# Macaron block with a Mamba2 scan on one core: gate tanh ahead of norms in the opening, the maxima's bank free with their copy, gate weights counted apart, conv copies ahead of the second norm

## The reference

```python
x = x + 0.5 * ffn(layernorm(x))          # first FFN
x = x + block(layernorm(x))              # h = y + mamba2(rmsnorm(y)), then h + mlp(rmsnorm(h))
x = x + 0.5 * ffn(layernorm(x))          # closing FFN, same weights

def ffn(x):    # W = (q - zeros) * scales in groups of 64, 512 x 512
    return x @ W.T + (x @ lora_A.T) @ lora_B.T / 16 + bias
def mamba2(h):
    z, xBC, dt = split(h @ w_in.T)       # 512 | 128 + 128 + 512 | 4 columns
    xBC = silu(causal_conv_4_taps(xBC) + conv_b); dt = softplus(dt + dt_bias)
    Y = scan over chunks of 128 tokens, 4 heads, state 128 x 128 per head
    return ((Y + D * x) * silu(z)) @ w_out.T
def mlp(h):
    return (silu(h @ gate_w.T) * (h @ up_w.T)) @ down_w.T      # 1792 wide
```

## Time and profile before

| | before |
|---|---|
| median of 3 runs | 795.04 us (794.87 to 795.27) |
| profiled execution | 794.72 us |
| span in its trace | 793.0 us |
| mean granted clock of TensorE | 0.987 |
| PE busy | 762.4 us, 96% |
| DVE, ACT, POOL busy | 628.0, 448.0, 335.8 us |

### The profile page before, as it was taken

The page is one execution under the profiler, slowest core; times in us unless marked ns, Lnnn a source line. Parts: engine busy times, 40 slices in busy tenths (PEclk is TensorE's granted clock), DMA queues, the critical chain, the costliest instruction groups (busy, mean ns, idle before and its releaser), DMA issues.

```text
span 793.0 us, 10650 instructions
## 1 busy us (share of the span) xinstructions
PE 762.4 (96%) x3470; PEld 355.1 (45%) x3470; DVE 628.0 (79%) x1235; ACT 448.0 (57%) x881; POOL 335.8 (42%) x392
## 2 busy tenths in 40 slices
PE   8899799999999889989997999999999999999998
PEld 3444354454455445434443444444444444444443
DVE  7798568978867877787799787887878878767994
ACT  4876656776775756544436455545645555534441
POOL 5631334563543268764614125125224224223674
PEclk9999899999999989999999899999999999999999
DMA  8832653542331111620151354644544643443655
GB/s 303 182 67 53 136 91 79 94 107 54 80 68 27 41 27 27 126 41 20 31 129 28 80 119 72 129 100 82 139 81 80 146 80 68 79 81 67 120 159 133
DMA packets 95415, 71.86 MB, mean 91 GB/s; under 512 B 65233, under 2 KB 72401, under 8 KB 95361
## 3 DMA queue, kind: packets, MB, share of 16 engines
q0 software_dynamic: 17280, 31.46, 22.2%
q1 hardware_dynamic: 77600, 39.66, 20.0%
q10 hardware_dynamic: 480, 0.07, 0.1%
HBM read 20.32 MB, written 4.19 MB: 31 GB/s over the span
## 4 chain that ended last, share of the span: by engine, by line
PE 70%; DVE 15%; ACT 6%; issue 3%; POOL 3%; DMA 2%; ACTq 0%; DVEq 0%; POOLq 0%
PE PS L1936 61%; PE PS L2059 3%; DVE raw L1447 2%; DVE st L1278 1%; PE PS L2067 1%; DVE state L1429 1%; PE PS L2158 1%; DMA x_t<-hb 1%; PE PS L2032 1%; PE PS L2041 1%; DVE w_in L1545 1%; ACT xds L833 1%; DVE stage L1447 1%; POOL r L520 1%; DVE xs L1379 1%
## 5 line engine op out<-in xcount | busy, mean ns | idle before, releaser
L1936 PE MATMUL PS<-h,w_in 128*128 128x512 f16 x480 | 111.5, 385 | 7.2 <-DVEq L1503 4.4
L711 POOL DMA_DIRECT2D xs<-x x59 | 50.9, 863 | 153.1 <-ACT x L1151 139.4
L1936 PE MATMUL PS<-h,x_t 128*128 128x512 f16 x408 | 94.0, 379 | 0.2 <-DVE pre L1780 0.2
L1936 PEld LDWEIGHTS PS<-h,w_in 128*128 128x128 f16 x480 | 47.3, 99 | 74.7 <-issue 18.3
L1936 PE MATMUL PS<-n_T,stage 128*128 128x512 f16 x288 | 71.5, 379 | 0.0
L1151 ACT ACTIVATE x<-PS,d_d 128x512 f32<-128x512 f32 x59 | 40.2, 681 | 38.6 <-PE PS L1936 38.6
L1936 PEld LDWEIGHTS PS<-h,x_t 128*128 128x128 f16 x408 | 39.5, 98 | 48.9 <-issue 2.7
L520 POOL TENSOR_TENSOR r<-mv,mhalf 128x1 f32<-128x1 f32 (+1 forms) x32 | 28.5, 891 | 70.6 <-DVE mv L1282 54.1
L711 POOL DMA_DIRECT2D xs<-n x29 | 25.2, 869 | 74.7 <-ACT n L1151 65.2
L1121 ACT ACTIVATE xds<-tm,dgh 128x512 f32<-128x512 f32 x24 | 17.3, 722 | 56.7 <-DVE tm L1867 56.7
L1936 PE MATMUL PS<-pre,stage 128*128 128x512 f16 x192 | 49.3, 379 | 0.0
(11 more groups left out here) (314 smaller groups left out, 1812.4 us busy)
## 6 DMA issues: line engine op xcount, KB each, us to landing
xs<-x POOLq DMA_DIRECT2D x75, 256.0 KB, 3.3
xs<-n POOLq DMA_DIRECT2D x29, 256.0 KB, 3.3
x_t<-x_in SPq DMA_DIRECT2D x16, 256.0 KB, 3.0
x_t<-hb POOLq DMA_DIRECT2D x16, 256.0 KB, 3.8
out<-x_t SPq DMA_DIRECT2D x16, 256.0 KB, 2.3
raw_gu<-gate_t SPq DMA_DIRECT2D x7, 512.0 KB, 4.4
raw_gu<-up_t SPq DMA_DIRECT2D x7, 512.0 KB, 6.5
raw_d<-down_t SPq DMA_DIRECT2D x7, 512.0 KB, 7.7
```

Source lines behind the costliest of these rows:

```text
L711: po.dma_start(chunk_of(xs, c), d_tmps[d % 3], accum_op=ALU.add).then_inc(s_acc[d % 3], 16)
L1936: ins = pe.matmul(out_, lhs(a, b, k), rhs(a, b, k), start=first and n == 0, stop=last and n == len(todo) - 1)
```

## The change

Five edits of order and counting; no operation on data is added or removed.

1. In the opening, ACT takes `hi0(8)` and the tanh of the gate blocks earlier, ahead of the norm `hi1(7)`; DVE takes `lo0(8)` and `silu_z` earlier, ahead of `lo1(6)` and `lo1(7)`.
2. Also in the opening, DVE's `max_row(1)` stands ahead of `x1_stats(3)`.
3. The bank of the first pair's maxima is freed by the copy out of it (`scale_read`, first count of e_scx) and no longer by the end of `scales` (e_wscale). The copy stands in step 10 ahead of `lo2` and `advance` on DVE, and `bound_spread(0)` ahead of `w(10)` and `csm(3)` on PE.
4. In steps 2, 6 and 10 ACT's conv copies (`slot_a` of the slot's first block) stand ahead of `hi1`, `scan2` and `renorm`.
5. For pairs 1 to 6 the gate weights are counted apart: ACT counts the high half of the gate by itself, DVE makes its low half in `st_g` and the other low halves in `st_a`, which in the last unit of a pair stands after the unit's u4 and c22 sums; PE waits for the gate at IP1 and for the rest at IP6.

```diff
@@ -285,6 +285,7 @@
+        W_HI_G = [4 * p - 1 for p in range(NP)]
@@ -307,7 +308,7 @@
             if c == 2 * CH + 2:
-                put(("mx", 0), (e_wscale, 1))
+                put(("mx", 0), (e_scx, 1))
@@ -945,6 +946,8 @@ ACT, step(c)
                     scan_decay(c + 1, (c + 1) % CH)
+                if j == 2 and i + 1 < NS:
+                    slot_a(i + 1, SLOTS[j][0])
                 if a < NCH:
                     hi1(a, a % CH)
@@ -955,7 +958,8 @@ ACT, step(c)
                 if i + 1 < NS:
-                    slot_a(i + 1, SLOTS[j][0])
+                    if j != 2:
+                        slot_a(i + 1, SLOTS[j][0])
                     slot_b(i + 1, SLOTS[j][0])
@@ -994,15 +998,15 @@ ACT, prologue
                 tanh(0, 4)
+                hi0(8, 0)
                 tanh_z(0, 0)
                 tanh(0, 5)
+                tanh_z(0, 1)
                 scan_ecs(0, 0)
                 scan1(0, 0)
                 scan_decay(0, 0)
-                hi0(8, 0)
+                tanh_z(0, 2)
                 hi1(7, 3)
-                tanh_z(0, 1)
-                tanh_z(0, 2)
                 scan2(0, 0)
                 tanh_z(0, 3)
@@ -1067,7 +1071,9 @@ ACT, hi_st
                     ac.wait_ge(e_norm, p)
-                    ac.activation(g[:, 0, :, :], raw_gu[:, 0, :, cols], ACT.Copy)
+                    first = ac.activation(g[:, 0, :, :], raw_gu[:, 0, :, cols], ACT.Copy)
+                    if x == 0:
+                        first.then_inc(e_w_hi, 1)
@@ -1486,17 +1492,15 @@ DVE, the scales of a pair
...
+            def scale_read(p):
+                ve.wait_ge(e_all, 2 + p + 1)
+                scale_link(p, itertools.count(1))(ve.tensor_copy(mxa3[:, :], PS[:, mx_bank(p), P:P + 3]))
@@ -1523,22 +1527,31 @@ DVE, the low halves
...
+            def st_g(p):
+                ve.wait_ge(e_w_hi, W_HI_G[p])
+                lo_g(0).then_inc(e_w_gu0, 1)
             def st_a(p):
-                ve.wait_ge(e_w_hi, p * 3)
-                lo_st(0).then_inc(e_w_gu0, 1)
+                ve.wait_ge(e_w_hi, W_HI_G[p] + 1)
+                lo_sums(0).then_inc(e_w_gu0, 1)
@@ -1634,16 +1647,16 @@ DVE, prologue
                 silu(0, 4)
+                lo0(8, 0)
                 silu_z(0, 0)
                 silu(0, 5)
+                silu_z(0, 1)
+                prep0(9, 1)
                 lo1(6, 2)
-                lo0(8, 0)
                 weights(0, 0)
-                silu_z(0, 1)
+                silu_z(0, 2)
+                scan1(0, 0)
                 lo1(7, 3)
-                silu_z(0, 2)
-                prep0(9, 1)
-                scan1(0, 0)
                 silu_z(0, 3)
@@ -1677,6 +1690,8 @@ DVE, step(c)
+                if c == 2 * CH + 2:
+                    scale_read(0)
                 if c > 0:
                     lo2(c - 1)
@@ -1751,8 +1766,8 @@ DVE, opening
+            max_row(1)
             x1_stats(3, 3, B_P[1])
-            max_row(1)
@@ -1847,16 +1863,19 @@ DVE, unit(m)
                     if n == 3:
-                        st_a(p + 1)
+                        st_g(p + 1)
...
                 ve.tensor_tensor(c22[k], u3[k], p_bank(m, IP5), ALU.add).then_inc(e_add, 1)
+                if p + 1 < NP and n == 3:
+                    st_a(p + 1)
@@ -2126,10 +2147,11 @@ PE, step(c)
+                if c == 2 * CH + 2:
+                    bound_spread(0)
                 w(c)
                 if c == 2 * CH + 2:
                     csm(i + 1)
-                    bound_spread(0)
@@ -2280,7 +2302,7 @@ PE, unit(m)
                 if x == 0:
-                    pe.wait_ge(e_w_gu0, p + 1)
+                    pe.wait_ge(e_w_gu0, 2 * p)
@@ -2291,6 +2313,8 @@ PE, unit(m)
+                if x == 0:
+                    pe.wait_ge(e_w_gu0, 2 * p + 1)
                 seventh(m, IP6)
```

More of the change, by code:

```diff
@@ L1487, in bound_row, with scale_link @@
                 ve.tensor_scalar(mdg[:, :], ident[0:3, 0:3], mr[:, :], None, ALU.mult).then_inc(e_max1, 1)
-            def scales(p):
[L1490 to L1499, removed]
+            def scale_link(p, n):
+                return lambda ins: link(ins, e_scx, p * 5 + next(n))
+            def scale_read(p):
+                ve.wait_ge(e_all, 2 + p + 1)
+                scale_link(p, itertools.count(1))(ve.tensor_copy(mxa3[:, :], PS[:, mx_bank(p), P:P + 3]))
+            def scales(p):
+                power_of_two(pw3[:, :], sw3[:, :], mxa3[:, :], scale_link(p, itertools.count(2)))
                 if p > 0:
@@ L1516, in dn_lo @@
             def dn_lo(p):
-                ve.wait_ge(e_w_hi, p * 3 + 2)
+                ve.wait_ge(e_w_hi, W_HI_G[p] + 3)
                 hi, lo_ = (w_dn[p % 2][:, a, :, :] for a in range(2))
@@ L1524, in cut_b, with lo_g, lo_sums @@
                 dn_lo(0)
-            def lo_st(x):
+            def lo_g(x):
+                cols = slice(x * P, (x + 1) * P)
+                g = w_st[x][0]
+                return ve.tensor_tensor(g[:, 1, :, :], raw_gu[:, 0, :, cols], g[:, 0, :, :], ALU.subtract)
+            def lo_sums(x):
                 cols = slice(x * P, (x + 1) * P)
                 g, u, s_ = w_st[x]
-                ve.tensor_tensor(g[:, 1, :, :], raw_gu[:, 0, :, cols], g[:, 0, :, :], ALU.subtract)
-                ve.tensor_tensor(u[:, 1, :, :], raw_gu[:, 1, 2:4, cols], u[:, 0, :, :], ALU.subtract)
                 for n in range(2):
                     ve.tensor_tensor(s_[:, 1, n, :, :], s_tmp[n][:, :, cols], s_[:, 0, n, :, :], ALU.subtract)
-                return ve.tensor_tensor(s_[:, 1, 2:4, :, :], s34[:, :, :, cols], s_[:, 0, 2:4, :, :], ALU.subtract)
+                ve.tensor_tensor(s_[:, 1, 2:4, :, :], s34[:, :, :, cols], s_[:, 0, 2:4, :, :], ALU.subtract)
+                return ve.tensor_tensor(u[:, 1, :, :], raw_gu[:, 1, 2:4, cols], u[:, 0, :, :], ALU.subtract)
+            def st_g(p):
+                ve.wait_ge(e_w_hi, W_HI_G[p])
+                lo_g(0).then_inc(e_w_gu0, 1)
             def st_a(p):
-                ve.wait_ge(e_w_hi, p * 3)
-                lo_st(0).then_inc(e_w_gu0, 1)
+                ve.wait_ge(e_w_hi, W_HI_G[p] + 1)
+                lo_sums(0).then_inc(e_w_gu0, 1)
             def st_b(p):
-                ve.wait_ge(e_w_hi, p * 3 + 1)
-                lo_st(1).then_inc(e_w_gu1d, 1)
+                ve.wait_ge(e_w_hi, W_HI_G[p] + 2)
+                lo_g(1)
+                lo_sums(1).then_inc(e_w_gu1d, 1)
             def t_lo(q, r_):
@@ L1831, in unit @@
                 if p + 1 < NP and n == 2 and m > 2:
+                    scale_read(p + 1)
                     scales(p + 1)
@@ L1859, in unit @@
                     t_los(3, 0, 1, 2, 3)
+                    scale_read(2)
                     scales(2)
@@ L1897, in _ @@
             gate_up(0, EARLY_GU)
+            scale_read(1)
             scales(1)
@@ L1903, in _ @@
             down(0)
+            st_g(1)
             st_a(1)
```

## The result

| | before | changed |
|---|---|---|
| median | 795.12 us (794.87 to 795.27, 4 runs) | 782.76 us (782.02 to 784.74, 4 runs) |
| ratio | | 0.9849, 95% interval 0.9829 to 0.9868 |
| profiled execution, its span | 794.72, 793.0 us | 782.24, 780.5 us |
| mean granted clock | 0.987 | 0.998 |

The account below looks back on a forecast made before the run. PE, busy 96% of the span, was taken as the bound, with gains only in its pauses and clock. 4.6 + 0 + 0.1 + 3.3 + 5.0 = 13.0 off 794.72 gives 781.7, plus 0.3 for the median 782.0; range 777.5 to 787.0.

Parts of the forecast that it names:

- Which pauses cost clock: PE's pauses: four, of 2.20 to 4.43 us, cost about twice their waits; behind shorter ones no half clock.
- Opening: Opening up to the next stage's product: f(8) starts at 89.7, scores' pause gone, one clock fall charged; gain 4.6 us.
- one fall of the clock: Opening, behind the remaining 2.0 us pause before f(8): a 3.4 us stretch at half clock, costing 1.7 us.
- The rival without a fall: Opening: the 2.0 us pause before f(8) costs no clock; 14.7 us gained in all, 780.3 us; chance 25%.
- The early maximum: Opening, row maximum ahead of x1_stats(3): the pause only moves to ACT's norm of chunk 5; gain 0.
- half clock through close pauses: Early maximum: pauses before 36.92 and before the next product come close enough for a clock fall; 1.7 us to lose.
- Conv copies: Steps 2, 6 and 10: earlier ACT copies hardly help, as full DVE frees the next bank; 0.1 us, between 0 and 2.7.
- The maxima's bank: Step 10: the 4.43 us wait and half clock vanish, partly given back with DVE then the limit; gain 3.3 us.
- The heirs that were named: Behind step 10: PE then waits about 0.9 us on cs_b, and later on POOL's scores.
- The gate: Before pair 2: pause down 2.1 us to 1.5, and 2.9 us of half clock back; gain 5.0 us.
- Sum: Whole kernel: the five terms add to a gain of 13.0 us, giving a median of 782.0 us.

Follow-up runs that it names:

- the pause filled: Changed kernel with ten matmuls computing nothing needed in the pause before f(8), into the bank f(8) then overwrites: 781.42 us, ratio 0.9833.
- the scales later: Changed kernel with scales and descale of the first pair behind the copies of the decays on DVE in step 10: 783.90 us, ratio 0.9860.
- the opening alone: Kernel before with only the new order of the opening (part 1), plus a piece of part 5: 789.91 us, ratio 0.9931.

## Why the prediction was right, point by point

- **Which pauses cost clock.** The argument that the long pauses are worth about twice what their waits say held: of the 12.5 us of span 6.2 are busy time of PE. But "four pauses cost, the shorter ones don't" is a reading of one execution. Other executions show 2.65 without half clock, and 1.72, and even 1.20 followed by 0.69, with it, while the 1.5 before pair 2 and the 1.7 and 1.5 on residual2 have none in any profile. Where a page of the Trainium skill (TensorE: Matmul & The Clock Gate, section Why this matters for your kernels) speaks of gaps over about 3 us, the runs have half clock behind pauses of 1.2 to 2.7 in some executions.
- **Opening, 4.6 forecast, 4.1 measured.** The steps came as written: the bank free early, then the transpose last; the scores no longer waited for; 3.5 from there to the next product (94.52 to 97.99); one fall of the clock, 1.7 as charged (4.45 for 2.75). The term that was mis-sized is the start of `f(8)`, 89.7 forecast, 90.24 measured: SP issued at 86.10, as counted (86.2), but its issue took 2.26 and not 1.23, and PE could start 4.1 after it began and not 3.5. In the two runs in which this issue took 1.23 (the pause filled, the scales later) it was 3.7 and 3.4. The pause was thus 2.7, not 2.0. The rival without a fall did not come true in the profile, and the mean clocks of 0.997 and 0.998 leave no execution of the four without half clock; with SP's order changed the pause itself is gone.
- **The early maximum, 0.** In the changed profile PE's eight matmuls began at 31.63 and not 33.38, and the wait of 1.20 on ACT's norm took it back as forecast. What was feared, half clock through close pauses, came in two of the nine profiles with the new order and in three of the five with the old one. That the old order could be the worse one stood nowhere in the prediction; the 0 may leave out up to 1.5 us of the 12.4, which is not shown.
- **Conv copies, 0.1.** Nothing at the end, shown by undoing them; in steps 2 and 6 residual2 was last, as argued. That they also take away a pause of 1.67 in step 10 the prediction didn't have.
- **The maxima's bank, 3.3 forecast, 3.2 measured.** Alone it gave 4.0, with 1.2 of uncertainty. The heirs that were named are in the profile, 0.70 for 0.9 on `cs_b` and the scores, and one that wasn't, the silu. residual2(11) went from 297.58 to 290.59, 7.0, less the opening's 4.1: 2.9; POOL's norm from 299.12 to 292.11, 2.9 for 3.0. Both are the forecast's numbers, but the count under them doesn't hold. It had 14 instructions and 13.4 us of work on DVE from 281.3 to residual2. The windows of that stretch before, and of the same stretch in the changed kernel (busy us of PE, PEld, DVE, ACT, POOL), have 22 instructions and 11.1 us, and 11.5 us:

```profile
281.31:297.58 16.27, 16.27 (x63) 7.61 (x62) 11.09 (x22) 9.44 (x21) 10.61 (x10) 0.89 0.16 33
```

```profile
277.13:290.59 13.46, 12.89 (x54) 6.27 (x55) 11.51 (x22) 9.21 (x21) 9.37 (x9) 1.00 0.20 40
```

The stretch now takes 13.46 because DVE also waits in it, 1.9 in all on ACT's tanh. So DVE was not full there, and that the 2.9 came out right was in part luck. The scales' place showed that of the first wait, once removed, two thirds go into the next one.
- **The gate, 5.0 forecast, 5.2 measured.** 2.1 of pause, the rest half clock. The clock's share hangs on the execution compared: behind a pause of 3.14 in the opening alone it would have been 1.7.
- **Sum.** 13.0 forecast, 12.5 in the profiles, 12.4 between the medians. The upper end of the range, 787.0, stands for a gain of 8 us and so for losses of 5 of the 13, not of 8 as written there.

## What to carry to other kernels

When an engine waits, write down who is last once that wait is gone, with its time from its own queue: here the transpose on SP, DVE and POOL behind step 10, and the gate's low half gave three gains to within 0.5 us each, one of them through a count that was wrong. A pause of TensorE of 1.7 to 3 us costs half clock in some executions; so one profile says what it cost once, and the way to be safe is to remove the pause, or at need to fill it. And a wait that moves from one releaser to another of the same length, as before `f(8)`, shows where the next edit belongs: swapping two triggers in SP's queue, together with one low half, was worth 4.7 us.

## What the runs showed of the hardware

- The same pause, another clock: 2.64 us and then twelve matmuls in 4.33 in one execution, 2.65 and 2.75 in another; 1.72 and then eight matmuls in 3.70, 5.39 or 5.40. Matmuls whose result is overwritten keep the clock up as others do (2.76 for twelve behind them).
- In the fourteen profiles half clock stood behind every pause of 3.1 us and more, behind nine of eleven pauses of 2.4 to 3.5 before `f(8)`, behind three of five of 1.72 near 33 us, and behind none of the pauses of 1.5 before pair 2 (nine profiles) and of 1.7 and 1.5 on residual2 (seven profiles).
- The issue of one transposing DMA on SP took 1.23 us mostly, and that of a load 0.58. Three issues lead up to `f(8)`: the transpose of chunk 6, a load and the transpose of chunk 8. In each of the nine profiles with the opening's new order and SP's old one, one of the three took longer: that of chunk 8 in seven (1.92 to 2.26, among them the changed kernel), that of chunk 6 in the pause filled, the load in the scales later:

```profile
84.08 2.32 SPq L443 DMA_TRANSPOSE h<-hn_p  x1
...
87.12 1.23 SPq L443 DMA_TRANSPOSE n_T<-n_p  x1
```

```profile
86.76 2.11 SPq L400 DMA_DIRECT2D x_t<-x_in  x1
88.97 1.23 SPq L443 DMA_TRANSPOSE n_T<-n_p  x1
```

With SP's order changed none of the three did (1.23 to 1.30, 0.57). What makes one longer was not found; it delays everything behind it in the queue, by 0.7 to 1.5 us here.
